# Second half of group 3 parted into heads and tails in a fused group norm and attention kernel

## The reference

```
y   = group_norm(x, 4 groups) * gamma + beta
q, k, v = split(w_qkv @ y + b_qkv)
w   = softmax(q^T k * C**-0.5)                 # 1024 x 1024 per batch
out = x + w_out @ (w @ v) + b_out
```

## Time and profile before

| | us |
|---|---|
| median of 3 runs | 134.29 (133.88 to 134.31) |
| the profiled execution's own time | 134.68 |
| its span | 132.9 |
| PE busy | 126.7 (95%) |
| DVE busy | 103.6 (78%) |
| POOL busy | 82.0 (62%) |
| ACT busy | 80.7 (61%) |
| DMA issue to landing, squares (92 issues) | 2.4 median |

### The profile page before, as it was taken

One profiled execution on the slowest core, in us unless ns is written; L12 is line 12 of the kernel. 1 busy time (PEld: TensorE's weight loads), 2 busy tenths in 40 slices (PEclk: granted clock), 3 DMA queues, 4 the chain that ended last, 5 costly groups with the idle time before them and its releaser, 6 DMA issues.

```text
span 132.9 us, 1913 instructions
## 1 busy us (share of the span) xinstructions
PE 126.7 (95%) x578; PEld 91.7 (69%) x578; DVE 103.6 (78%) x197; ACT 80.7 (61%) x140; POOL 82.0 (62%) x81
## 2 busy tenths in 40 slices
PE   6899989999999999999999999999998999999991
PEld 6787677777777566666765656776666778759890
DVE  0679886999999999769998785698886789667121
ACT  3066768776589656765963184579763895876000
POOL 5053175589448877973387678934999479843400
PEclk9999999999999999999999999999999999999999
DMA  4870000000039718993598759873899295952121
GB/s 152 273 284 2 0 5 0 0 2 0 0 70 205 165 41 192 205 207 109 118 209 195 194 115 201 199 199 72 189 210 223 59 202 117 200 158 79 39 83 40
DMA packets 6874, 16.65 MB, mean 125 GB/s; under 512 B 1872, under 2 KB 2128, under 8 KB 6864
## 3 DMA queue, kind: packets, MB, share of 16 engines
q1 hardware_dynamic: 6864, 16.53, 50.4%
HBM read 2.36 MB, written 2.10 MB: 34 GB/s over the span
## 4 chain that ended last, share of the span: by engine, by line
PE 55%; DVE 20%; POOL 12%; issue 5%; DMA 3%; ACT 2%; SPq 0%; DVEq 0%; POOLq 0%; ACTq 0%
PE mixed L927 16%; DVE scores L663 9%; DVE crossed L690 6%; PE scores L862 6%; PE scores L863 6%; PE scores L867 6%; POOL probs L367 5%; PE turned L881 3%; DMA xs<-in_x_dram 3%; POOL result L362 3%; POOL home_of_group L262 2%; PE turned L809 2%; POOL y_lo L343 2%; PE mixed L809 2%; DVE stats L578 2%
## 5 line engine op out<-in xcount | busy, mean ns | idle before, releaser
L367 POOL TENSOR_SCALAR probs<-probs,inv_sum 128x1024 f32<-128x1024 f32 x32 | 36.0, 1125 | 29.9 <-DVE inv_sum L668 29.7
L663 DVE TENSOR_SCALAR_CACHE_REDUCE scores<-scores,key_bias 128x1024 f32<-128x1024 f32 x31 | 39.9, 1287 | 8.6 <-PE scores L867 8.4
L462 ACT ACTIVATE probs<-scores,neg_max 128x1024 f32<-128x1024 f32 x32 | 35.7, 1117 | 17.4 <-DVE scores L663 16.6
L862 PE MATMUL scores<-y_hi,z_hi 128*128 128x512 f32 x62 | 33.3, 537 | 0.1
L690 DVE STREAM_TRANSPOSE crossed<-probs 128x1024 f32<-128x1024 f32 x24 | 29.8, 1242 | 1.5 <-POOL probs L367 1.4
L927 PE MATMUL mixed<-crossed,v 128*128 128x512 f32 x64 | 30.3, 593 | 0.0
L863 PE MATMUL scores<-y_lo,z_hi 128*128 128x512 f32 x62 | 24.4, 394 | 0.0
L867 PE MATMUL scores<-y_hi,z_lo 128*128 128x512 f32 x62 | 19.3, 392 | 0.0
L927 PEld LDWEIGHTS mixed<-crossed,v 128*128 128x128 f32 x64 | 11.6, 190 | 8.3 <-issue 7.2
L862 PEld LDWEIGHTS scores<-y_hi,z_hi 128*128 128x128 f32 x62 | 11.7, 188 | 7.9 <-issue 4.9
L863 PEld LDWEIGHTS scores<-y_lo,z_hi 128*128 128x128 f32 x62 | 11.7, 189 | 6.4 <-issue 4.8
(11 more groups left out here) (179 smaller groups left out, 212.9 us busy)
## 6 DMA issues: line engine op xcount, KB each, us to landing
crossed<-crossed SPq DMA_DIRECT2D x92, 128.0 KB, 2.4
out_dram<-result SPq DMA_DIRECT2D x7, 256.0 KB, 2.4
xs<-in_x_dram SPq DMA_DIRECT2D x4, 256.0 KB, 3.5
xs<-in_x_dram SPq DMA_DIRECT2D x2, 512.0 KB, 6.3
ws<-in_weights_dram SPq DMA_DIRECT2D x1, 256.0 KB, 3.7
out_dram<-result SPq DMA_DIRECT2D x2, 128.0 KB, 1.9
vecs<-in_vectors_dram SPq DMA_DIRECT2D x1, 3.0 KB, 3.4
```

The source lines that it names most:

```text
L367: pool.tensor_scalar(probs[:, i % RING, :], probs[:, i % RING, :], inv_sum[:, i:i + 1], 1.0, ALU.mult, ALU.mult).then_inc(s_probs, 1)
L462: act.activation(probs[:, i % RING, :], scores[:, i % 2, :], ACT.Exp, bias=neg_max[:, i:i + 1], scale=-1.0, accum_out=row_sum[:, i:i + 1]) ...
L663: dve.tensor_scalar(scores[:, i % 2, :], scores[:, i % 2, :], key_bias[:, b % 2, i:i + 1], None, ALU.subtract, ALU.min, accum_out=neg_max[ ...
L862: pe.matmul(to[h], z_hi[:, b % 2, query], y_hi[:, b % 2, halves[h]], start=True, stop=False)
```

## The change

Pairs 2 and 3 of group 3 (its tiles 4 to 7) become parted tiles. The second half of batch 1's values gets a head, by one ScalarE copy of 128x512 in stage 17, and a tail, by one VectorE subtraction in the same stage. In stage 19 ScalarE copies the heads of both pairs. The tail of pair 2 is made by VectorE in stage 20, behind the flip, and that of pair 3 by GpSimd in stage 21, ahead of the normalising of block 23; both are written in place over the fp32 tiles. The tiles per stage of group 3 go from (3, 2, 1, 2) to (3, 1, 2, 2). The diff, without the declarations of the new semaphores:

```diff
+    EARLY_PARTED = {2: "vector", 3: "gpsimd"}
-        for k, tiles in enumerate((2, 2, 2, 2) if group == 5 else (3, 2, 1, 2) if group % 2 else (1, 2, 3, 2)):
+        for k, tiles in enumerate((2, 2, 2, 2) if group == 5 else (3, 1, 2, 2) if group == 3 else (3, 2, 1, 2) if group % 2 else (1, 2, 3, 2)):
...
+        early_v_hi, early_v_lo = sb("early_v_hi", [128, KT // 2, C], fp32r), sb("early_v_lo", [128, KT // 2, C], fp32r)
+        early_heads = sb("heads_of_group_3", [128, 2, N], fp32r)
...
+        def early_tail(engine, k):
+
+            engine.wait_ge(s_early_heads, k - 1)
+            engine.tensor_tensor(pair_of_tiles(flat(tails_6), k), pair_of_tiles(crossed[:, HOME[3], :], k),
+                                 squares_by_query(early_heads[:, k - 2, :]).bitcast(fp32),
+                                 ALU.subtract).then_inc(s_early_tails[EARLY_PARTED[k]], 1)
...
+                    if BLOCKS * b + i == 21:
+                        early_tail(pool, 3)
...
+                    if BLOCKS * b + i == 17:
+                        act.wait_ge(s_v, 6)
+                        act.activation(early_v_hi[:, :, :], v[:, 1, KT // 2:KT, :], ACT.Copy).then_inc(s_early_v_hi, 1)
+                    if BLOCKS * b + i == 19:
+                        act.wait_ge(s_swapped[1], swaps(3))
+                        for k in EARLY_PARTED:
+                            act.activation(squares_by_query(early_heads[:, k - 2, :]),
+                                           pair_of_tiles(crossed[:, HOME[3], :], k), ACT.Copy).then_inc(s_early_heads, 1)
...
+                    if BLOCKS * b + i == 20:
+                        early_tail(dve, 2)
...
+                    if BLOCKS * b + i == 17:
+                        dve.wait_ge(s_v, 6)
+                        dve.wait_ge(s_early_v_hi, 1)
+                        dve.tensor_tensor(early_v_lo[:, :, :], v[:, 1, KT // 2:KT, :], early_v_hi[:, :, :].bitcast(fp32),
+                                          ALU.subtract).then_inc(s_early_v_lo, 1)
...
-                    if (group, k // 2) in MID_NUMBER:
+                    if group == 3 and k // 2 in EARLY_PARTED:
+                        pe.wait_ge(s_early_v_lo, 1)
+                        pe.wait_ge(s_early_tails[EARLY_PARTED[k // 2]], 1)
+                        head = early_heads[:, k // 2 - 2, :].rearrange("p (g v u c) -> p v u g c", g=SQ, v=2,
+                                                                       u=QB)[:, k % 2, :, :, :]
+                        tail = tile_by_query(flat(tails_6), k)
+                        pe.matmul(bank, early_v_hi[:, k - KT // 2, :], head, start=False, stop=False)
+                        pe.matmul(bank, early_v_hi[:, k - KT // 2, :], tail, start=False, stop=False)
+                        mm = pe.matmul(bank, early_v_lo[:, k - KT // 2, :], head, start=False, stop=final)
+                    elif (group, k // 2) in MID_NUMBER:
```

More of the change, by code:

```diff
@@ L193, in attention_kernel @@
         s_diagonal = {"scalar": sem("diagonal_by_scalar_copied"), "gpsimd": sem("diagonal_by_gpsimd_copied")}
+        s_early_v_hi = sem("early_v_head_ready")
+        s_early_v_lo = sem("early_v_tail_ready")
+        s_early_heads = sem("heads_of_group_3_ready")
+        s_early_tails = {"vector": sem("group_3_tails_by_vector_ready"), "gpsimd": sem("group_3_tails_by_gpsimd_ready")}
         s_mid_v_hi = sem("mid_v_head_ready")
```

## The result

The changed kernel takes 135.68 us (median of 6 runs), the kernel before 134.30 us in the same session: ratio 1.0105, 95% interval 1.0087 to 1.0122. It is 1.38 us slower; 135.3 us had been forecast. Its profiled execution has an own time of 135.6 us and a span of 133.8.

The account below looks back on a forecast made before the run. TensorE was taken to bound stages 19 to 22, other engines near. After 0.64 us saved, 1.7 us of new waiting left stage 22 1.04 us late: 134.29 + 1.0 = 135.3 us, range 133.7 to 136.0.

Parts of the forecast that it names:

- Step 1: Stage 17: ScalarE's copy and VectorE's subtraction (0.61 to 0.75 us) fit in idle gaps; price 0, at most 0.1 us.
- Step 2: Stage 19: ScalarE's two head copies, 0.95 to 1.05 us each, delay z_hi by 0 to 0.13 us; taken as 0.
- Step 3: Stage 20: VectorE's tail of pair 2, behind block 21's flip, takes 1.22 to 1.35 us, ending at 85.05 to 85.2.
- Step 4: Stage 21: TensorE waits for VectorE's tail; with 0.38 and 1.40 us after it, the stage ends at 86.9, before 86.62.
- Step 5: Stage 20: GpSimd's z tail loses 0.95 us beside VectorE's two-input subtraction (bounds 0 and 1.3), ending at 86.15.
- Step 6: GpSimd's tail of pair 3 ends at 89.65; group 5's transfers begin some 1.2 us later, at price 0.
- Step 7: Stage 22: TensorE waits for GpSimd's tail and ends at 91.43 against 90.39, 1.04 us late.
- Nothing given back: After stage 22: no later slack on TensorE, GpSimd or ScalarE, so the 1.04 us delay reaches the kernel's end.
- only the queue is late: Rival: GpSimd loses nothing beside VectorE's tail; stage 22 ends at 90.7, 0.3 us late, total 134.6; chance 0.2.
- Late, but taken back: Rival: a later wait, above all GpSimd's stretch from 107.17, returns 1.0 to 1.6 us: 133.8 to 134.4; chance 0.08.
- worse: Rival: contended time moves on to the residual, or group 5's transfers land too late: over 136.0 us; chance 0.05.
- The saving is kept: Rival: both tails arrive before TensorE asks in stages 21 and 22, keeping the 0.64 us saving: 133.6; chance 0.17.

Follow-up runs that it names:

- e8: Changed kernel with VectorE's tail of pair 2 ahead of the flip of block 21 and group 2's residual behind the normalising of block 23: 134.63 us, ratio 1.0041.
- e1: Changed kernel without both new tails of group 3; TensorE reads the heads in their place: runs of 134.97 and 135.29 us, no ratio taken.
- e12: Kernel before with e6's parting of pair 2, residuals 3 and 4 behind normalising of blocks 27 and 30, store 3 among group 6's transfers: 134.13 us, ratio 0.9993.
- e5: Kernel before with residual 3 moved behind the tail of stage 25 and residual 4 behind the normalising of block 30: 134.62 us, ratio 1.0030.
- e9: Kernel before with GpSimd's residual of group 4 alone moved, behind the normalising of block 30: 133.94 us, ratio 0.9981.
- e11: Kernel before with residuals 3 and 4 behind the normalising of blocks 27 and 30, store 3 between group 6's 12th and 13th transfers: 134.31 us, ratio 1.0002.
- e6: e5 plus only pair 2 of group 3 parted, VectorE's tail ahead of the flip, residual 2 at the end of stage 20: 134.86 us, ratio 1.0038.
- e10: e6's parting of pair 2, with residual 3 back in stage 23 and residual 4 behind the normalising of block 30: 134.06 us, ratio 0.9995.
- e4: Changed kernel with GpSimd's residual of group 2 moved from stage 19 to behind the normalising of block 23: 135.05 us, ratio 1.0060.

## Why the prediction was right, and which step of it was wrong

The verdict, the kind of mechanism (VectorE's two-input subtraction beside GpSimd) and roughly the size were right: 1.0 us late was forecast, 1.38 measured. Which engine loses, and so the split of TensorE's waiting, was not. That the total held all the same is partly luck: the normalising of block 22, with GpSimd's whole queue behind it, stands behind the z tail and behind VectorE's reciprocal, so that a microsecond lost on either engine makes it about as late.

- *Step 1, stage 17 free.* Wrong in its row: the subtraction took 1.33 us, not 0.61 to 0.75. GpSimd's normalising ran until 73.96, 0.79 us into it, which the step left out (without it, by the rule of the last section, 0.69 us, an estimate), and the y instruction behind it then took 1.62 (1.20 before). The maximum of block 20 came 0.5 us later from the mark (74.42 less 76.72, against 74.36 less 77.17). TensorE paid nothing for it up to the scores that end at 80.85.
- *Step 2, heads free.* Right, 0.00.
- *Step 3, VectorE's tail.* Two errors. It began 0.37 us later than forecast, since the maximum of block 22 began 4.62 us after the mark, not 4.25, and it took 2.25 us, not 1.22 to 1.35.
- *Step 4, TensorE's wait in stage 21.* The terms hold: 0.39 us from the tail's end (85.96) to the steady pieces (86.11 and 0.24), as against 0.38, and 1.40 for the pair. With step 3's error the wait was 1.66, not 0.5.
- *Step 5 is the one that failed.* It priced the contention rightly (0.95 forecast, 1.03 measured) and put it on the wrong engine. Both rows that it rested on, 3.05 and 2.25 us, have GpSimd as the one that starts later; I read them as "GpSimd loses beside VectorE". The instruction that starts later loses, whichever engine it is on. Here that was VectorE, by 0.11 us. In the forecast's own times VectorE was the earlier, 83.87 against 83.92, but by 0.05 us only, and nothing was said of the order. By the same reckoning, had VectorE's maximum not been 0.37 us late, its tail would have started 0.26 us ahead of the z tail and GpSimd would have paid; e8, in which VectorE starts 0.36 us ahead, shows this, but with the residual moved too.
- *Step 6, GpSimd late.* Right by another way: the normalising of block 22 waited for VectorE's reciprocal, which stood behind the long tail (GpSimd idle 1.25 us), rather than for a slow z tail. From the mark GpSimd's tail ended at 89.61 less 76.72, 12.89 us; forecast was 89.65 less 77.17, 12.48. These 0.41 us (0.37 of them the late maximum) are what the forecast lacks to the measured 1.47 at the end of stage 22. The transfers of group 5 cost nothing, as put.
- *Step 7.* The end of stage 22 is the tail's end, 0.38 and 1.40, as put (89.61, 91.41). But TensorE had already been held in stage 21, so 0.22 us of waiting was left here, not over 1.
- *Nothing given back.* Right in the changed kernel: 1.47 at stage 22, 1.49 at the turning of blocks 28 and 31, 1.38 at the end.

One reading ahead of the steps was wrong too: GpSimd does not work without a pause until 86.3 us, it idles 0.73 us before 80.35. No step rests on it.

Of the rivals, "only the queue is late" had a z tail of 1.3 us as its sign, and the z tail did take 1.28 us. The sign was badly chosen, since it looked at GpSimd alone: what the rival says, that nothing is lost to contention, is false. VectorE's tail took 2.25 us, the reciprocal of block 22 ended 9.31 us after the mark and not 8.08 (85.25 less 77.17), and the time is 1.1 us over that rival's 134.6. "Late, but taken back" and "worse" did not come: 1.38 of 1.47 us are left at the end, and 136.0 is not passed. "The saving is kept" fails twice over. e1 shows that without any tail the saving still ends in the wait for GpSimd at 102 us, a term that the prediction's second rival did not have. e12 shows that behind this the transfers of group 6 are next. TensorE's 95% was an average: close behind its own work stand GpSimd's queue from 92 to 102 us (0.47 us of waiting before the change) and the flip of block 27 with its 16 transfers, which in e12 took back all but 0.04 of the 0.71 us that block 31 had gained.

Open: why VectorE's maximum of block 22 starts 0.49 us after the scores end (80.85 to 81.34; before 81.30 to 81.42). All runs with the instructions of stages 17 and 19 have 4.62 or 4.63 us from the mark, those without them (before, e5, e9, e11) 4.25 or 4.26. It is so too in e6, e10 and e12, which have one head copy, ended well before. Neither a wait nor an instruction in the records accounts for it, and no run took stage 17's part away alone. Open too is why the 16 issues of group 6 take 10.87 us in e9's profile and 11.63 in that of before, a difference larger than the gains looked for.

## What to carry to other kernels

Before you give VectorE a two-input SBUF instruction, find what GpSimd runs at that moment: the one that starts second is longer by the remainder of the first (here less 0.15 us), and everything queued behind it is late by that. In this kernel a gap on an idle engine was worth only what lay in it at the right moment; and a saving on the busiest engine was worth at most the smallest slack of the engines that feed it, which one run with the feeding left out (e1) shows before the feeding is written.

## What the runs showed of the hardware

A VectorE instruction with two SBUF inputs and a GpSimd instruction hardly ran beside each other. In every pair of these runs that overlapped by more than 0.15 us the one that started later took its own time, plus what was left of the other, less 0.15 us (fitted to these rows):

| later one | alone | left of the other | sum less 0.15 | measured |
|---|---|---|---|---|
| GpSimd tail, before | 2.41 | 0.79 | 3.05 | 3.05 |
| GpSimd residual, before | 1.28 | 1.10 | 2.23 | 2.25 |
| VectorE tail 1024 at 111.05, before | 1.22 | 0.28 | 1.35 | 1.35 |
| VectorE tail 1024, changed | 1.22 | 1.17 | 2.24 | 2.25 |
| VectorE tail 1024, e4 | 1.22 | 0.48 | 1.55 | 1.57 |
| GpSimd z tail, e8 | 1.28 | 0.86 | 1.99 | 1.99 |
| VectorE tail 1024, e1 | 1.22 | 2.38 | 3.45 | 3.47 |
| GpSimd tail, e10 | 2.41 | 1.19 | 3.45 | 3.46 |
| GpSimd y (one tensor input), changed, stage 17 | 1.20 | 0.55 | 1.60 | 1.62 |

An overlap of 0.11 us cost nothing (VectorE's tail behind a normalising in e6, 1.22 us). The earlier one did not pay. It kept its time in seven of the nine rows; in those of GpSimd's residual and y the earlier one was a VectorE subtraction that had itself started behind GpSimd's normalising. So the 1.35 us of the earlier trace rows is the same rule, with this row of the kernel before:

```profile
110.21 1.12 POOL L367 TENSOR_SCALAR probs<-probs,inv_sum 128x1024 f32<-128x1024 f32 x1
```

That row and the last of the table show that GpSimd's instruction need not have two inputs. The order is decided by hundredths: before, VectorE's tail started 0.43 us ahead and GpSimd's lost 0.64 us; in e1 VectorE's started 0.02 us behind and lost 2.25. GpSimd's instructions beside VectorE's maxima and flips kept their times (2.41 at 99.82). The Trainium skill ("GPSIMD Engine Reference", 1. Specifications) names the contention for VectorE's two-SBUF-input instructions; which engine waits and for how long is from these rows.
